# Routing of the last token groups ahead of the first expert slots, and two square roots behind the last silu, in a fused scan and mixture-of-experts kernel

## The reference

```python
x = x + _layernorm(attn(_layernorm(x), Wi, bi, Wr, br, cap_lambda))   # x: 16 x 256 x 128
x = x + _layernorm(ffn(_layernorm(x), gate_w, w1, w3, w2, e_bias))

# attn: a gated linear recurrence along the 256 steps of each sequence
it = sigmoid(x @ Wi.T + bi); rt = sigmoid(x @ Wr.T + br)
at = exp(-8.0 * softplus(cap_lambda) * rt)
gx = sqrt(1.0 - at ** 2) * (it * x)
h[t] = at[t] * h[t-1] + gx[t]

# ffn: 32 experts (128 -> 96 -> 128), the best 4 for each token
scores = sigmoid(x @ gate_w.T)
topk_ids = top_k(scores + e_bias, 4)
topk_w = scores[topk_ids] / sum(scores[topk_ids])
out = sum over e of (silu(x @ w1[e]) * (x @ w3[e]) * combine[:, e]) @ w2[e]
```

## Time and profile before

| What | Value |
| --- | --- |
| Median of three runs | 338.76 us |
| The profiled execution's own time | 340.02 us |
| Its span, first to last instruction | 338.2 us |
| Mean granted TensorE clock | 0.909 of full |
| Busy: PE | 272.8 us (81%) |
| Busy: VectorE (DVE) | 250.5 us (74%) |
| Busy: GpSimd (POOL) | 238.4 us (70%) |
| Busy: ScalarE (ACT) | 215.5 us (64%) |
| Chain that ended last: PE, POOL, issue, DVE | 35%, 32%, 12%, 10% |

### The profile page before, as it was taken

How to read it: one execution, slowest core, us unless ns; L and a number is a source line. 1 busy time by engine, 2 the same in 40 slices (tenths; PEclk the granted TensorE clock), 3 DMA queues, 4 the chain that set the end, 5 groups by cost and what they waited for, 6 DMA issues and landing times.

```text
span 338.2 us, 6619 instructions
## 1 busy us (share of the span) xinstructions
PE 272.8 (81%) x1531; PEld 220.3 (65%) x1532; DVE 250.5 (74%) x953; ACT 215.5 (64%) x561; POOL 238.4 (70%) x273
## 2 busy tenths in 40 slices
PE   4976366675452989999999999999999999899930
PEld 2554243452341879889886998998967667799810
DVE  3789976787975487697446997854467897698796
ACT  6986687888713545556553555665458858875782
POOL 4398677778777777777763777777767777777710
PEclk9999787876755899999999999999999999999965
DMA  4999999951113455667745899988532112251232
GB/s 114 326 302 287 282 274 301 296 153 49 54 47 97 132 176 175 186 198 224 218 129 146 206 263 260 243 225 218 140 85 52 48 50 53 54 148 49 55 101 63
DMA packets 83999, 54.81 MB, mean 162 GB/s; under 512 B 8032, under 2 KB 80512, under 8 KB 83968
## 3 DMA queue, kind: packets, MB, share of 16 engines
q1 hardware_dynamic: 57472, 30.85, 33.5%
q0 software_dynamic: 6912, 14.17, 14.9%
q10 hardware_dynamic: 19584, 9.44, 9.8%
HBM read 25.07 MB, written 29.36 MB: 161 GB/s over the span
## 4 chain that ended last, share of the span: by engine, by line
PE 35%; POOL 32%; issue 12%; DVE 10%; ACT 4%; DMA 4%; SPq 1%; POOLq 0%; ACTq 0%; DVEq 0%
POOL xs_dram L438 32%; PE bank L1841 6%; PE bank L1829 6%; PE bank L1761 6%; PE bank L1832 5%; PE bank L1797 4%; DMA xb<-xs_dram 2%; PE bank L1778 2%; PE bank L1756 2%; DMA wi_raw<-in_L_attn_Wi_dram 1%; DVE st L792 1%; DVE yk L1437 1%; DVE hT L952 1%; ACT L680 1%; ACT yk L740 1%
## 5 line engine op out<-in xcount | busy, mean ns | idle before, releaser
L447 POOL DMA_INDIRECT yk<-ys_dram,row_ys x108 | 107.1, 992 | 39.0 <-issue 27.4
L438 POOL DMA_INDIRECT xs_dram<-xn_all,row_xs x108 | 109.2, 1011 | 35.2 <-issue 32.6
L1761 PE MATMUL bank<-w,xbT 128*128 x288 | 59.7, 331 | 0.0
L688 ACT COPY xbT<-bank 128x256 f32<-128x256 f32 x72 | 26.9, 373 | 35.4 <-PE bank L1756 33.8
L1203 DVE TENSOR_TENSOR act_a<-silu,bank 128x192 f32<-128x192 f32 x72 | 25.3, 351 | 28.0 <-ACT silu L691 26.5
L1797 PE MATMUL bank<-w2s,aT 96*128 x288 | 45.7, 281 | 0.1
L1761 PEld LDWEIGHTS bank<-w,xbT 128*128 128x128 f32 x288 | 45.7, 193 | 0.1
L1797 PEld LDWEIGHTS bank<-w2s,aT 96*128 96x128 f32 x288 | 37.8, 191 | 2.1 <-issue 1.7
L1756 PE MATMUL bank<-ident,xb 128*128 128x128 f32 x144 | 29.5, 282 | 9.8 <-DMA xb<-xs_dram 9.6
L691 ACT ACTIVATE silu<-bank 128x192 f32<-128x192 f32 x72 | 23.8, 331 | 18.4 <-PE bank L1761 17.7
L1212 DVE COPY yb<-bank 128x256 f32<-128x256 f32 x72 | 30.3, 421 | 6.0 <-PE bank L1797 5.2
(11 more groups left out here) (234 smaller groups left out, 530.2 us busy)
## 6 DMA issues: line engine op xcount, KB each, us to landing
xb<-xs_dram SPq DMA_DIRECT2D x144, 64.0 KB
ys_dram<-yb ACTq DMA_DIRECT2D x72, 128.0 KB
xs_dram<-zeros SPq DMA_DIRECT2D x2, 2048.0 KB, 15.1
ys_dram<-zeros SPq DMA_DIRECT2D x1, 2816.0 KB, 14.0
ys_dram<-zeros SPq DMA_DIRECT2D x1, 2560.0 KB, 17.2
x_sb<-in_L_attn_x_dram SPq DMA_DIRECT2D x8, 256.0 KB, 5.2
xs_dram<-xn_all,row_xs POOLq DMA_INDIRECT x108
yk<-ys_dram,row_ys POOLq DMA_INDIRECT x108, 2.5
```

The costliest lines, as they stand in the source:

```text
L438: pool.indirect_dma_start(out=xs[h], out_offset=bass.IndirectOffsetOnAxis(ap=row_xs[:, j, k:k + 1], axis=0), in_=xn2_all[:, j, :], in_offs ...
L447: pool.indirect_dma_start(out=yk[h][:, j - h * TP, k, :], out_offset=None, in_=ys[h], in_offset=bass.IndirectOffsetOnAxis(ap=row_ys[:, j, ...
L688: act.copy(xbT[:, p, :, :].rearrange("c b t -> c (b t)"), ps_xbT[p][:, 0:2 * P]).then_inc(b_xc[h], 1)
L1761: ins = pe.matmul(ps_gu[o][:, b * 2 * I:(b + 1) * 2 * I].rearrange("t (w a i) -> t w a i", w=2, a=1), xbT[:, o, b, :], w13[:, :, bass.ds(e ...
```

## The change

Three places are changed. First, groups 5 to 7: ScalarE's and VectorE's `last()` and TensorE's program ahead of the first slot now hold the turning of groups 6 and 7, the logits of group 6, the scores of groups 5 and 6, and the choice of group 5. The rest (`logits` and `score` of group 7, the choice of groups 6 and 7, `positions`, `rows`, the tables of half 1) moves to earlier calls of `slot`. `chosen` gets a wait for the rows of the group before. Second, the early pieces: 0, 1 and 2 before slot 0 of half 1, 3 before slot 1, none before slot 2. Third, the end: the square roots 1 and 2 go behind the last silu, behind the load that was there; the normalizations that hang on them go after them; two of the weightings of group 6 go into pieces 44 and 46.

```diff
-        EARLY, EARLY_AT = 4, [(0, 1), (2,), (3,)]
+        EARLY, EARLY_AT = 4, [(0, 1, 2), (3,), ()]
...
@@ ScalarE, last() @@
 
+                act.preload_act_table(ACT.Tanh)
+                score(G - 3)
+                act.preload_act_table(ACT.Sqrt)
                 std_h(G - 1)
                 std_1(G - 2)
                 norm_h(G - 1)
+                turned_1(G - 2)
                 std_1(G - 1)
+                act.preload_act_table(ACT.Silu)
+                score(G - 2)
+                turned_1(G - 1)
...
             def late(t):
 
                 if t == 0:
-                    act.preload_act_table(ACT.Silu)
-                    score(G - 3)
-                    turned_1(G - 2)
+                    score(G - 1)
                     most.append(steps_value(act, 0))
-                if t == 2:
-                    score(G - 2)
-                    turned_1(G - 1)
-                if t == 3:
-                    score(G - 1)
...
@@ ScalarE, between(e) and behind the pieces @@
                 if e in (31, 33, 35, 37):
                     weighted(5, (e - 31) // 2)
-                if e == 42:
-                    root_last(1)
-                    root_last(2)
-                if 44 <= e < 48:
-                    norm_last(4 + (e - 44) // 2, 1, e % 2)
+                if e in (44, 46):
+                    weighted(6, (e - 44) // 2)
...
             act.preload_act_table(ACT.Sqrt)
-            for j in range(by_act(6)):
-                weighted(6, j)
+            root_last(1)
+            root_last(2)
+            for n in range(2):
+                norm_last(4, 1, n)
             turned_back(1)
             for j in range(by_act(7)):
                 weighted(7, j)
             root_last(3)
+            for n in range(2):
+                norm_last(5, 1, n)
             root_last(4)
...
@@ VectorE, chosen(e) @@
                 dve.wait_ge(v_pick, 3 * e + 3)
+                ge(dve, v_val, e)
...
@@ VectorE, last() @@
                 norm_1(G - 1)
+                best(G - 3)
+                take_out(G - 3)
+                chosen(G - 3)
...
@@ VectorE, aside(h, t) @@
                 elif t == 0:
-                    best(G - 3)
+                    best(G - 2)
+                    take_out(G - 2)
                 elif t == 1:
-                    take_out(G - 3)
-                    chosen(G - 3)
+                    rows(G - 3)
+                    chosen(G - 2)
                 elif t == 2:
-                    packed_rows(0, 0)
-                elif t == 3:
-                    best(G - 2)
-                elif t == 4:
-                    take_out(G - 2)
-                    chosen(G - 2)
-                elif t == 5:
                     rows_cast(G - 3)
                     best(G - 1)
-                elif t == 6:
                     take_out(G - 1)
+                elif t == 3:
                     chosen(G - 1)
...
@@ VectorE, between(e) and behind the pieces @@
-                if e == 43:
-                    inverse_last(1)
-                if e == 44:
-                    inverse_last(2)
-                    norm_d(0)
-                if e == 45:
-                    add_d(0)
...
             weigh_in_6(3)
-            add_last(4)
-            add_last(5)
             two_sums(6, by_act(6))
+            inverse_last(1)
+            inverse_last(2)
...
+            norm_d(0)
+            add_d(0)
+            add_last(4)
...
@@ TensorE, ahead of the first slot and in slot @@
+            turn_1(G - 2)
+            logits(G - 2)
+            turn_1(G - 1)
             pe.wait_ge(a_ti, G)
...
                 if h == 0 and isinstance(t, int) and t == 0:
-                    turn_1(G - 2)
+                    logits(G - 1)
                 if h == 0 and isinstance(t, int) and t == 1:
-                    turn_1(G - 1)
-                if h == 0 and isinstance(t, int) and t == 2:
-                    logits(G - 2)
-                if h == 0 and isinstance(t, int) and t == 3:
-                    logits(G - 1)
+                    positions(G - 3)
```

More of the change, by code:

```diff
@@ L1260, in ahead @@
             def ahead(t):
-                if t in (3, 5, 7):
-                    rows(G - 3 + (t - 3) // 2)
-                if t in (9, 11, 13):
-                    tables(1, (t - 9) // 2)
-                if t == 14:
+                if t in (3, 5):
+                    rows(G - 2 + (t - 3) // 2)
+                if t in (7, 9, 11):
+                    tables(1, (t - 7) // 2)
+                if t == 12:
                     tables(1, 3)
@@ L1287, in aside @@
                 elif t == 0:
-                    best(G - 3)
+                    best(G - 2)
+                    take_out(G - 2)
                 elif t == 1:
-                    take_out(G - 3)
-                    chosen(G - 3)
+                    rows(G - 3)
+                    chosen(G - 2)
                 elif t == 2:
-                    packed_rows(0, 0)
-                elif t == 3:
-                    best(G - 2)
-                elif t == 4:
-                    take_out(G - 2)
-                    chosen(G - 2)
-                elif t == 5:
                     rows_cast(G - 3)
                     best(G - 1)
-                elif t == 6:
                     take_out(G - 1)
+                elif t == 3:
                     chosen(G - 1)
-                elif t == 8:
+                elif t == 4:
                     rows_cast(G - 2)
-                elif t == 9:
+                    packed_rows(0, 0)
+                elif t == 5:
                     rows_cast(G - 1)
                     scores_of(G - 1)
-                elif 10 <= t < 16:
-                    packed_rows(0, t - 9)
+                elif t in (6, 7, 8):
+                    packed_rows(0, t - 5)
+                elif t in (10, 11, 12):
+                    packed_rows(0, t - 6)
                 elif t > 15:
@@ L1493, in _ @@
                     spread_d(1)
+                    inverse_last(3)
                     dve.wait_ge(s_fourth, 16)
@@ L1713, in ahead @@
             def ahead(t):
-                if t in (3, 5, 7):
-                    positions(G - 3 + (t - 3) // 2)
-                if t in (9, 11, 13):
-                    tables(1, (t - 9) // 2)
-                if t == 14:
+                if t in (3, 5):
+                    positions(G - 2 + (t - 3) // 2)
+                if t in (7, 9, 11):
+                    tables(1, (t - 7) // 2)
+                if t == 12:
                     tables(1, 3)
+            turn_1(G - 2)
+            logits(G - 2)
+            turn_1(G - 1)
             pe.wait_ge(a_ti, G)
```

2 lines of the change are left out of this document (1 added, 1 removed).

## The result

| | Before | Changed |
| --- | --- | --- |
| Median, 22 runs each | 340.71 us (337.34 to 343.06) | 338.93 us (336.65 to 342.12) |
| Ratio, 95% interval | | 0.9952 [0.9932, 0.9971] |
| Profiled execution, its span | 340.02, 338.2 us | 337.95, 336.2 us |
| Mean granted clock | 0.909 | 0.906 |
| TensorE, VectorE, ScalarE, GpSimd busy | 272.8, 250.5, 215.5, 238.4 us | 275.5, 250.9, 216.0, 237.6 us |

The change saves 0.48%, 1.6 us. The forecast was 0.9 us less (0.27%), within 1%, and the time lies in its range; the gain is nearly twice the forecast's. Beside the median of 3 runs that the forecast started from, 338.76, the 338.93 would look like no gain: over 22 runs the kernel before has 2 us more. Only the ratio, from runs of both on the same chips, shows it.

What follows compares the result with a forecast made beforehand. Bound: GpSimd's scatters and block loads until about 181 us, then TensorE, with VectorE ending the tail. Terms -1.30 - 0.41 + 1.4 - 0.6 = -0.9 us took 338.76 to 337.9 us, range 335.4 to 339.5.

Steps and rivals of the forecast that it cites:

- The lead, 4.2 us: Half 0's slots on TensorE: end 4.2 us earlier (from 3.15 to 5.3), at 173.7 instead of 177.88.
- Pieces 0 to 2 hidden, one piece off the path, -1.30: Before half 1's slot 0: three early pieces done at 177.8; one piece left between slots 0 and 2, minus 1.30 us.
- The wait at slot 4, -0.41: Half 1's early slots: TensorE's wait at 189.61 goes as VectorE does call 0's side work while waiting, 0.41 us.
- The clock, +1.4: Before half 1's slot 0: TensorE idles 2.9 us, its clock falls until about 186, costing 1.4 us.
- the forecast's likeliest case: Whole kernel: the clock falls before half 1's slots and 1.4 us is paid; 337.9 us, chance 0.48.
- the first rival: Before half 1's slots: the clock holds, the 1.4 us are not paid, minus 2.3 us, 336.5; chance 0.27.
- The tail, -0.6: End of kernel: silus follow TensorE without loads among them, VectorE ends at 335.1; minus 0.7 us, taken as 0.6.
- The wait for the roots that was the upper bound: Tail: VectorE waits once for the root behind the load, plus 0.5 us.
- The 2.09 of the lower bound: Tail: VectorE's whole idle time of 2.09 us is won, minus 2.1 us.
- "Stays low": Half 1's first slots: the clock falls and stays low until 190.5, losing 4.4 us; 340.9, chance 0.07.
- "No lead": Half 0 ends less than 1.3 us earlier, piece 2 isn't hidden, only the tail gains; 338.2, chance 0.08.
- The signs: Forecast wrong if last scatter moves over 1 us, half 1's first slot isn't 5 us from it, or VectorE awaits roots.

Runs made afterwards that it cites:

- warm_front: Changed kernel with 12 and 8 idle transposes around the work ahead of half 0's first slots; 0.9987 of the kernel before.
- after_again: The changed kernel itself, timed and profiled again on the chip of later runs; 0.9936 of the kernel before.
- warm_four: warm_front with all four early pieces ahead of slot 0 of half 1; 0.9955 of the kernel before.
- fill_on_scatter: warm_front with 6 idle transposes, a wait for half 1's scatters and 10 more before half 1's slot 0; 0.9947 of the kernel before.
- w2_loads_later: Changed kernel with the four w2 loads for the dense pieces moved behind SP's steps 2 to 5; 1.0007 of the kernel before.
- front_early: Kernel before with the routing of groups 5 to 7 and the early pieces moved, tail as before; 0.9942 of the kernel before.
- front_only: Kernel before with only the routing of groups 5 to 7 moved ahead; 0.9985 of the kernel before.
- w2_loads_out: Changed kernel without the four w2 loads for the dense pieces and the wait for them; 0.9895 of the kernel before.
- the three w2 kernels: w2_loads_later, w2_loads_out and w2_loads_in_parts: changed kernel with four w2 loads moved later, left out or split; 1.0007, 0.9895 and 1.0057 of the kernel before.
- early_only: Kernel before with only the early pieces moved ahead of slots 0 and 1; 1.0011 of the kernel before.
- w2_loads_in_parts: Changed kernel with the same w2 bytes over the same four steps in 16 loads of 96 KB; 1.0057 of the kernel before.
- fill_gap: Changed kernel with 16 idle transposes between the early pieces and slot 0 of half 1; 0.9946 of the kernel before.

## Why the prediction was right, and where it wasn't

**The lead, 4.2 us: too large by about one.** Half 0's slots ended 2.26 us earlier than before in the profile. They did get shorter, 70.30 us (107.58 to 177.88) before and 67.05 after, 3.25 less, near the lower bound of 3.15. That is the longest of the eight profiles with the new routing and no fill in the front: they took 66.29 on average, and the three with the old routing 70.29, so 4.0 less, near the 4.2. But they also began later, 1.0 us in the changed kernel's profile. Measured from the last scatter, the eight have the slots' end 0.55 us ahead of S on average, from 0.87 behind to 1.56 ahead; the three had it 2.57 behind (2.15, 2.15 and 3.40): a lead of 3.1 us on average. The step that failed is the start: the forecast took 4.2 off the end at 177.88 and let slot 0 begin where it had. Why its blocks came later is open; in the changed kernel's profile TensorE waited for them, and SP had begun to load when it had before.

The clock in the front was hardly in the forecast, beyond one set of logits at the low level. It rose within 114 to 118 in all eight, and within 112 to 113 in the three: with the work moved ahead, the slots had the low clock for longer. What that cost isn't measured by itself; with the clock up from 108 on (warm_front) the slots of half 0 took 63.25 us.

**Pieces 0 to 2 hidden, one piece off the path, -1.30: right.** S to slot 2 fell by 1.94 and 2.04 in the two profiles. In after_again 1.31 of it is the piece: from the second block to slot 2 it took 185.54 - 181.34 = 4.20 us before and 2.89 there. The other 0.73 is that the second block came sooner behind S, 4.88 us against 5.61, which the forecast didn't have.

**The wait at slot 4, -0.41: wrong.** It is 0.56 in the changed kernel, and a wait of 0.21 to 0.72 stands in every profile but warm_four's. It isn't left-over work of call 0, as I had it, but side work of a later call, ahead of the product on VectorE. The chain of fill_on_scatter goes through it, from wsel to hot, 1.96 us:

```profile
186.64 0.21 DVE wsel L1140
...
188.01 0.59 DVE hot L1131
188.60 0.27 DVE act_a L1208
```

**The clock, +1.4: the mechanism is shown, its price at slot 2 was low, and both profiles of the changed kernel don't pay it.** Where the clock fell it cost 1.68. In the two profiles it held: TensorE stopped for 0.17 us in one and for 0.94 + 0.23 in the other, since the lead was small. It fell after 1.48 + 0.74 (w2_loads_later), 1.65 + 0.44 (front_early), 2.00 + 0.24 (front_only) and 2.97 + 0.36 us (warm_front), and held after 1.69 + 0.43 (w2_loads_out). So the forecast's likeliest case was wrong by its own observable, and the first rival, "the clock holds", is what the profile shows. It isn't so in every execution: of the six profiles with the changed kernel's program on TensorE in this place (its own two, front_early and the three w2 kernels) the clock fell in two. By that, an estimate of the mean price is 1.68 x 2 / 6 = 0.6 us.

**The first rival's size, -2.3 us, wasn't reached either,** since the slots of half 1 gave back 1.75 and 0.98 us in the two profiles. This term was missing: I let everything behind slot 2 follow the start one for one. With the w2 loads out it does follow (58.99 us), so the loads in front of blocks have a part in it. With these loads in place, kernels whose slot 2 came 7.7 to 8.3 us after S took 60.6 to 62.3 us (five profiles), and those with 9.6 to 11.0 took 59.3 to 60.3 (six). So from S to piece 4 the changed kernel has won only 0.19 and 1.06 us. Why the same loads cost less when the slots start later is open.

**The tail, -0.6: right, 0.92 measured.** VectorE ends its products at 320.04 + 0.42 = 320.46, 1.47 us after the last pair's end at 318.99; the forecast had 321.7 - 320.17 = 1.53, and before it was 4.25. What follows took 13.2 us, where the forecast had 13.4 and it was 11.37 before. The wait for the roots that was the upper bound didn't come. The 2.09 of the lower bound wasn't near: of the 2.78 us gained up to the products, 1.86 went into the work that moved behind them.

**By sum.** Forecast -1.30 - 0.41 + 1.4 - 0.6 = -0.9. By the profiles, from S: -1.94 + 1.75 - 0.01 - 0.92 = -1.12, and -2.04 + 0.98 - 0.01 - 0.92 = -1.99 (after_again), 1.6 on average, as the timed runs say; with one profile of before and two of the changed kernel, 0.9 apart, so close an agreement is in part luck. The total was near for a partly wrong reason: a cost that was mostly not paid stood in for a giving back that I hadn't seen.

**The other rivals, and the tables.** "Stays low" didn't occur: each low stretch seen ended before 186. "No lead" is nearly early_only, where piece 2 wasn't hidden: 1.0011, without the tail. That a switch of tables costs 2.66 us (the Trainium skill, ScalarE: Activation LUTs, "What ACT_TABLE_LOAD costs") is again not what the trace has: the silu ends at 319.55, the load runs from 319.57 to 320.85, and the root begins at 320.87.

**The signs.** The last scatter moved by 0.98 and 1.84 us in the two profiles, one of them beyond the 1 us that was to prove the forecast wrong. Since it moves by 4.7 us over all kernels, the sign was badly chosen. The distance from it to half 1's first slot, which was to stay 5 us, is 5.01 and 4.32.

## What to carry to other kernels

A lead on an engine is worth only what is ready to be put into it. Of two edits of which one makes the lead and the other uses it, each may measure as nothing; try them together before dropping either. When work is moved into an idle place, ask what granted clock it leaves for what follows, and when a start is moved earlier, look for the bulk loads that share the queue with what the earlier work needs. For differences under one per cent, cut each profile at the same landmarks and compare stretch by stretch: the tail's 0.92 us was the same to 0.03 in all fourteen profiles while the timed ratio couldn't tell it from nothing.

## What the runs showed of the hardware

- The granted clock fell after a stop of 1.48 + 0.74 us and after one of 1.65 + 0.44, and held after one of 1.69 + 0.43, with the same program on TensorE: the sums of the stops, 2.2, 2.1 and 2.1 us, don't separate them. By the Trainium skill (TensorE: Matmul & The Clock Gate, "HAM oscillation — how this bites in real kernels") the price is half the length of the low stretch. In warm_front the windows from 180 to 184 have 0.66, 0.50, 0.50 and 0.63, low for about 3.4 of 4 us; half of that is 1.7, and 1.68 was measured: the trace agrees.
- A load of 96 KB costs SP's queue as much as one of 384 KB: 0.43 (w2_loads_in_parts, 191.30) and 0.42 us (the changed kernel, 186.72). The same bytes in 16 loads in place of 4 made the kernel slower: 1.0057 of the kernel before, where the changed kernel has 0.9952.
- Idle transposes of 128x128 cost 0.11 us each at the full clock (16 in 1.75 us, 181.36 to 183.11, fill_gap).
